# A smaller run-ahead for GpSimd's first gathers in a graph kernel: 8 until 24 are issued, and 24 until 44

## What is computed

```python
e = edge_attr @ eW + eb
m = jax.nn.relu(x[src] + e)
agg = jax.ops.segment_sum(m, dst, num_segments=N)
h = (1.0 + eps) * x + agg
return jax.nn.relu(h @ W1 + b1) @ W2 + b2
```

## Time and profile before

| | |
|---|---|
| median of 3 runs | 4527.47 us (4523.1 to 4533.64) |
| the profiled execution's own time | 4526.65 us |
| its span | 4525.0 us |
| PE busy | 2865.0 us (63%) |
| DVE busy | 2207.9 us (49%) |
| POOL busy | 1870.5 us (41%) |
| ACT busy | 726.2 us (16%) |
| line 831, gathers of the four message passes | 1056, mean 963 ns, 561.2 us idle before them |
| line 2267, gathers of the attention pass | 264, mean 1033 ns, 123.3 us idle before them |

### The profile page before, as it was taken

The page is one execution under the profiler, slowest core; times in us unless marked ns, Lnnn a source line. Parts: engine busy times, 40 slices in busy tenths (PEclk is TensorE's granted clock), DMA queues, the critical chain, the costliest instruction groups (busy, mean ns, idle before and its releaser), DMA issues. The chain is left out here.

```text
span 4525.0 us, 52039 instructions
## 1 busy us (share of the span) xinstructions
PE 2865.0 (63%) x16062; PEld 2374.0 (52%) x16063; DVE 2207.9 (49%) x4940; ACT 726.2 (16%) x1635; POOL 1870.5 (41%) x1982
## 2 busy tenths in 40 slices
PE   3566657775777667750568256767769639947492
PEld 2456545563565455540557123336758639936391
DVE  7566645554555545566246556771254421144213
ACT  1122112221222212210112000002210113300120
POOL 4566456664666366636315666711100020020212
PEclk8788877877777777875769566667979869968696
DMA  5733223332333233313423133317756459945693
GB/s 129 287 87 88 68 67 90 90 84 59 88 89 90 53 90 89 90 34 130 161 54 109 41 92 93 94 43 254 245 185 234 157 183 327 309 149 171 210 338 119
DMA packets 358089, 607.55 MB, mean 134 GB/s; under 512 B 82185, under 2 KB 240187, under 8 KB 355131
## 3 DMA queue, kind: packets, MB, share of 16 engines
q1 hardware_dynamic: 245816, 357.76, 24.3%
q0 software_dynamic: 88640, 214.25, 17.0%
q10 hardware_dynamic: 23363, 32.26, 2.0%
HBM read 508.28 MB, written 95.81 MB: 134 GB/s over the span
## 5 line engine op out<-in xcount | busy, mean ns | idle before, releaser
L831 POOL DMA_INDIRECT gine_got<-gine_table,src x1056 | 1017.4, 963 | 561.2 <-issue 271.4
L905 PE MATMUL gine_p_sum<-gine_hot,gine_got 128*128 128x128 f32 x4224 | 782.9, 330 | 204.5 <-issue 174.0
L905 PEld LDWEIGHTS gine_p_sum<-gine_hot,gine_got 128*128 128x128 f32 x4224 | 690.2, 240 | 289.8 <-issue 266.0
L957 DVE TENSOR_TENSOR gine_got<-gine_got,gine_p_edge 128x512 f32<-128x512 f32 x528 | 360.5, 683 | 601.5 <-DMA unpack_rows<-in_edge_rows 250.7
L916 ACT ACTIVATE gine_got<-gine_got 128x512 f32<-128x512 f32 x528 | 332.2, 630 | 1309.5 <-DVE gine_got L957 946.9
L940 DVE TENSOR_TENSOR stack_acc<-stack_acc,gine_p_sum 128x256 f32 x1056 | 437.6, 414 | 43.0 <-issue 1.5
L489 POOL DMA_INDIRECT adjacency<-value,place x264 | 280.3, 1062 | 390.3 <-POOLq L54 191.4
L892 PE MATMUL gine_p_edge<-gine_w_a,edge_space 128*128 128x256 bf16 x1056 | 329.1, 326 | 98.7 <-issue 94.1
L893 PE MATMUL gine_p_edge<-gine_w_b,edge_space 128*128 128x256 bf16 x1056 | 328.7, 325 | 98.9 <-issue 85.8
L1416 PE MATMUL ffn_p_h<-ffn_xt,ffn_w 128*128 128x128 f32 x2864 | 347.7, 280 | 1.7 <-DVE ffn_xt L1468 0.5
L1416 PEld LDWEIGHTS ffn_p_h<-ffn_xt,ffn_w 128*128 128x128 f32 x2864 | 337.5, 196 | 4.6 <-issue 2.5
(11 more groups left out here) (399 smaller groups left out, 3365.4 us busy)
## 6 DMA issues: line engine op xcount, KB each, us to landing
gcn_a<-adjacency SPq DMA_DIRECT2D x270, 320.0 KB
ffn_w<-in_L_ffn_W SPq DMA_DIRECT2D x74, 1024.0 KB
ffn_w<-in_L_ffn_w SPq DMA_DIRECT2D x60, 1024.0 KB
ffn_w<-in_L_ffn_w SPq DMA_DIRECT2D x90, 512.0 KB
adjacency<-zero_row ACTq DMA_DIRECT2D x3, 7200.0 KB
gine_got<-gine_table,src POOLq DMA_INDIRECT x1056
h_table<-score_rows SPq DMA_DIRECT2D x15, 1056.0 KB
edge_space<-dst_lines ACTq DMA_DIRECT2D x3, 2816.0 KB
```

The costliest lines, as they stand in the source:

```text
L831: pool.indirect_dma_start(got[:, c % RING, :], None, table, bass.IndirectOffsetOnAxis(ap=rows[:, c:c + 1], axis=0)).then_inc(gathered[c % ...
L905: ins = nc.tensor.matmul(p_sum[q % NB][:, k * D + half * P:k * D + (half + 1) * P], got[:, d % RING, half * P:(half + 1) * P], hot[:, d % ...
L957: nc.vector.tensor_tensor(both, both, p_edge[p % NB][:, :], ALU.add).then_inc(summed, 1)
```

## The change

No instruction is added, removed or moved on any engine. Only the counts change for which GpSimd waits before a gather, and 16 gathers of each message pass (chunks 8 to 23) and 20 of the attention pass (chunks 24 to 43) get a wait that they did not have. In a message pass gather c with 8 <= c < 24 waits until (c - 8) // 2 + 1 pairs are aggregated, from 24 on until (c - 24) // 2 + 1 are, as before. In the attention pass gather c with 24 <= c < 44 waits for c - 23 chunks, from 44 on for c - 43, as before.

```diff
 LAG = 4
 RING = 24
+OPEN = 8
 HOTS = 12
...
         if c >= RING and not couples:
             pool.wait_ge(used, c - RING + 1)
-        if c >= RING and couples:
-            pool.wait_ge(used, (c - RING) // 2 + 1)
+        if c >= OPEN and couples:
+            pool.wait_ge(used, (c - (RING if c >= RING else OPEN)) // 2 + 1)
         pool.indirect_dma_start(got[:, c % RING, :], None, table,
...
     W, L, K = Windows.COUNT, Windows.LANES, 8
-    HELD, SUMS = 44, 5
+    HELD, OPENED, SUMS = 44, 24, 5
...
-                if c >= HELD:
-                    pool.wait_ge(agg_done, c - HELD + 1)
+                if c >= OPENED:
+                    pool.wait_ge(agg_done, c - (HELD if c >= HELD else OPENED) + 1)
                 pool.indirect_dma_start(got[:, c % HELD, 0:FULL], None, h_table,
```

## The result

The changed kernel takes **4548.1 us** (median of 11 runs, 4537.9 to 4558.15), the kernel before, run beside it, 4523.1 us (11 runs, 4513.83 to 4533.64). The ratio is **1.0058, 95% interval 1.0047 to 1.0069**: slower by 25 us. The forecast was +20 on 4527, so 4547, with a range of 4495 to 4580. That the time lies only 1 us from it is partly luck: the kernel before came out 4 us lower beside the changed one than in the runs that the forecast started from.

What follows compares the result with a forecast made beforehand. Passes were taken to last as long as their gathers plus POOL's pauses at a nearly full ring. Passes 2 to 4 +1, pass 1 +19 and attention 0 gave +20 on 4527: 4547 us, range 4495 to 4580.

Steps and rivals of the forecast that it cites:

- PE's progress is held up while POOL issues without a pause, and comes free in POOL's pauses: All passes: unbroken gathers slow the consumers until the ring is full; pairs 4 and 5 lost 18.1 us in pass 2's opening.
- The stall moves, it does not go: Passes 2 to 4: the unbroken run comes after gather 24 instead of at the start; +0.3 us a pass, about +1 together.
- Pass 1, +19 us: Pass 1: 16 fewer slots filled during ScalarE's DMAs, so gather 50 starts at 226.1 instead of 207.01; bounds 0 and 24.
- Attention, 0: Attention pass: gather 72 starts at 2681 against 2681.86 before, taken as 0, bounds -12 and +12 us.
- the stall is one of a cold start: Rival, passes 2 to 4 and attention: the stall does not form again, giving 4451 us; chance 0.22.
- PE's pace is its own: Rival, all passes: the ring's run-ahead is only spare, so no change, 4527 us; chance 0.18.
- POOL's clock binds after the opening: Rival, passes 2 to 4: PE's slow opening is its own, gather 24 some 20 us later, near 4607 us; chance 0.07.

Runs made afterwards that it cites:

- the first four: Kernel before with the change in passes 2 to 4 plus attention, pass 1, or attention (4528.57, 4549.23, 4532.11 us), or passes 2 to 4 at most 8 ahead (4506.25).
- plain fetches: Kernel before, but in passes 2 to 4 SyncE fetches table-order rows by plain DMAs and POOL issues no gathers: 4025.6 us.
- free gathers: The plain fetches kernel plus 264 unread, unbroken POOL gathers a pass: 5037.9 us; repeated in pass 2 of the last experiment.
- gathers in fours: The free gathers kernel, but POOL waits for landing after every fourth gather: 4622.86 us; repeated on another chip as pass 4 of the last experiment.
- the last experiment: Changed kernel, but passes 2 to 4 use plain fetches and unread gathers: unbroken, paused every eighth, paused every fourth; 4783.39 us.
- the narrow rings: Kernel before, at most 8 gathers ahead in passes 2 to 4 (ratio 0.9956), at most 32 in attention (0.9965), or both together (1.0013).

## Why the prediction was right, point by point

**"PE's progress is held up while POOL issues without a pause, and comes free in POOL's pauses"**: the first half is shown on two chips: by plain fetches (1.75 us a pair, one chip), free gathers (33.6, both) and gathers in fours (1.75, the other), and in agreement with the traces of the chip of the first four. On one chip it does not hold. The second half is right for the pauses of these kernels, but PE comes free only behind a delay, of 4 us after 26 gathers and 26 us after 264. By the Trainium skill, SBUF — State Buffer, section Who interferes with whom, PE and ACT never wait on anyone; that section is about the ports of SBUF. PE's one matmul in 2.8 us beside unbroken gathers, against a whole pair in 1.75 beside gathers in fours, shows that PE is held on these chips, but no run shows it held at a port. So the rule is not refuted, and the prediction asked more of it than it says. Where the hold sits is not settled; what the traces show late is the raising of PE's semaphores. Landing bytes alone are excluded, since pass 4 of the last experiment takes more of them per us and runs free, and since pass 2's hold lasts 22 us beyond its last gather's bytes.

**"The stall moves, it does not go", +1 us for passes 2 to 4**: right in kind. Gather 24 starts 34.1 us after gather 0 (forecast 35.8), because gathers 8 and 16 end rounds of 11.8 us each and 24 finds its slot free at once: the round that begins with gather 16 runs on into the 16 new slots. So the run is gathers 16 to 43, 28 of them, not the 26 from 24 on. The closing pause is 4.81 us (4.4 forecast), gather 50 stands at 71.6 (72.7). Each pass ended 0.7 to 1.5 us earlier where 0.3 later was forecast; that is inside the bounds of -4 to +5 and too little to be told from no change.

**Pass 1, +19 us**: measured +21.2 in the trace, 22 by the run with this part alone. The term was right, but its working missed three times, and that the first two cancel is luck. Gather 8 is let go at 163.98, not at 168.21. Gather 24 comes at 191.1 all the same (forecast 191.9), since 16 and 20 wait another 6.22 and 1.24 us. The unbroken run is 22 gathers, 20 to 41, not 26, and the closing pause is 4.2 us where I took 1.7, so gather 50 comes at 229.0 (forecast 226.1). The timeline of POOL in pass 1, its gathers 8, 16, 20 and 42, beside the earlier trace rows:

```profile
163.98 0.94 POOL L832 DMA_INDIRECT gine_got<-gine_table,src  x1 [28.84 <-PE gine_p_sum L906]
...
180.11 0.95 POOL L832 DMA_INDIRECT gine_got<-gine_table,src  x1 [6.22 <-PE gine_p_sum L906]
...
186.06 0.94 POOL L832 DMA_INDIRECT gine_got<-gine_table,src  x1 [1.24 <-PE gine_p_sum L906]
...
217.53 0.94 POOL L832 DMA_INDIRECT gine_got<-gine_table,src  x1 [4.24 <-remote]
```

Why gather 8 comes early stands in ScalarE's row, which I had taken as fixed:

```profile
124.33 36.51 ACTq L473 DMA_DIRECT2D adjacency<-zero_row  x3
```

Its three DMAs take 36.51 us beside 8 gathers where they took 40.81 beside 24. The other two traces with the changed pass 1 have 36.5 too, and the eleven with 24 gathers there have 40.8 to 41.1, also on the chip without the hold. So filling the slots in ScalarE's time was cheap, not free: 16 gathers cost ScalarE's DMAs 4.3 us.

For the rest the mechanism is the one forecast: in the kernel before 24 slots are filled while ScalarE is busy with its own DMAs, and the change forbids 16 of these.

**Attention, 0**: this term was mis-sized. It is most of what the sum lacks: by the traces passes 2 to 4 came out 4 us under their term, pass 1 2 us over and attention 6 over, 24 in all for the forecast 20. It costs 6 us (438.2 against 432.2), 5 by the run alone. Gather 24 waits 3.00 us and starts at 32.8 us (forecast 32), gather 44 at 64.6 (64), gather 72 at 100.6 (102). But the run ends at 74 with a pause of 5.10 us, not 3, and VectorE's one long wait is 17.59 us where the earlier trace rows has 13.36 and 14.12. The timelines of POOL and of VectorE:

```profile
2623.39 0.95 POOL L2268 DMA_INDIRECT edge_space<-h_table,hrow  x1 [3.00 <-PE inorder_p_sum L2303]
...
2698.47 0.94 POOL L2268 DMA_INDIRECT edge_space<-h_table,hrow  x1 [5.10 <-PE inorder_p_sum L2303]
```

```profile
2694.00 0.25 DVE L2348 TENSOR_TENSOR inorder_less<-inorder_score,inorder_p_back 128x96 f32<-128x96 f32 x1 [17.59 <-DMA rank_every<-router_weights]
```

By gather 263 the delay is 2 us (384.1 against 382.1); the other 4 arise behind the last gather, and what sets them was not tried.

**The rivals.** That the stall is one of a cold start falls with 703.07 and 710.18 in the timeline above. That PE's pace is its own falls with the 1.75 us a pair of the plain fetches, on these chips. That POOL's clock binds after the opening falls with gather 24 at 34.1 us, not 57.

## What to carry to other kernels

A ring that is deep enough to let GpSimd issue some 20 gathers in one go can cost more than it buys: look for a stretch in which PE's rows say "issue" at 2 us a matmul while POOL has no pause, and try a ring that is just deep enough. In these kernels that was worth 7 us a pass. A pause after every fourth gather frees PE, but it makes 264 gathers last 466.6 us, more than the 405 us of the whole pass, so it pays only where gathers are not what the pass waits for; one after every eighth makes them last 398.5, which is about what the full ring does by itself. Neither was tried in a kernel that uses the gathered rows.

Never take run-ahead from a stretch in which the consumer can't start anyway: those slots are nearly free. And measure such a change on more than one chip before keeping it: the narrow rings were worth about 0.4% each where PE is held, and together cost 0.1% on the chip where it is not.

## What the runs showed of the hardware that I had not expected

- How strong the hold is: 33.6 us a pair beside unbroken gathers against 1.75 without, 19 times as long. PE's semaphore goes up 88 us after the matmul that raises it has started.
- How little a pause must be: one of 2.4 us in the mean after every fourth gather, beside 5.0 us of issuing, leaves nothing of the hold (1.75 us a pair). In rounds of eight it shows from some 8 us into the round on.
- That it goes on when GpSimd has stopped: 4 us after 26 gathers, 26 us after 264, with the last bytes landed 22 us before.
- That gathers also slow ScalarE's plain DMAs: 40.8 us beside 24 gathers, 36.5 beside 8.
- That it depends on the chip. The kernel before takes 4188 us on one and 4499 to 4527 on the others, and on that one POOL's unbroken gathers leave PE alone. The granted clock of the kernel before is higher there, 0.82 to 0.83 against 0.77 to 0.78, but the kernel with plain fetches reaches 0.82 on a chip with the hold (0.77 there for the kernel before), so the higher clock seems to go with a PE that is not held, rather than to free it. What differs between the chips is open.
- That the steady round is 8 gathers in 11.8 us whether the ring holds 8 slots or 24. Why it is just that is open too; the pass with spare gathers, paused after every eighth, does about 5 pairs in such a round (12.1 us at 2.3 us a pair), the real ones 4.
